# A state-space mixer with a mixture of experts: x added by an accumulating transfer, and sums of squares by four 32-column strips

## What is computed

```python
xn = layernorm(x)
zxbcdt = xn @ in_proj_w.T                    # z, xBC, dt
xBC = silu(conv_b + causal_conv4(xBC, conv_w))
theta = clip(theta_base + tanh(xn @ theta_w1) @ theta_w2)
lam = lambda_base + viscosity_eta * theta**2
# scan over chunks of 64 with state S: S_t = exp((-lam + i theta) dt) S_{t-1} + B_t x_t dt
y = real(C . S) + D * x_ssm
g = y * silu(z)
g = g * rsqrt(mean(g*g, over 512 features) + 1e-5) * norm_w
mixer = g @ out_proj_w.T
e_out = xn @ expert_w[idx] + expert_b[idx]   # idx: the router's best expert of each token
out = x + mixer + gate * e_out
```

## Time and profile before

| what | value |
|---|---|
| median of 3 runs | 1242.69 us (1236.13 to 1245.13) |
| the profiled execution's own time | 1231.05 us |
| its span in the trace | 1229.2 us |
| mean granted TensorE clock, share of full | 0.942 |
| PE busy | 1063.8 us, 87% |
| PEld busy | 826.3 us, 67% |
| DVE busy | 1044.4 us, 85% |
| ACT busy | 815.0 us, 66% |
| POOL busy | 270.0 us, 22% |
| DMA share of 16 engines, loop of the mixer | 0.44 |

### The profile page before, as it was taken

How to read it: one execution, slowest core, us unless ns; L and a number is a source line. 1 busy time by engine, 2 the same in 40 slices (tenths; PEclk the granted TensorE clock), 3 DMA queues, 4 the chain that set the end, 5 groups by cost and what they waited for, 6 DMA issues and landing times.

```text
span 1229.2 us, 26224 instructions
## 1 busy us (share of the span) xinstructions
PE 1063.8 (87%) x8826; PEld 826.3 (67%) x8827; DVE 1044.4 (85%) x1934; ACT 815.0 (66%) x1453; POOL 270.0 (22%) x307
## 2 busy tenths in 40 slices
PE   3772299846899999999999999999999999999895
PEld 2441266544677777777777777777877777777674
DVE  5757923227999999999999999999999999999962
ACT  2441211108988888887888888888888888887650
POOL 1212676600011111221111111111122111111111
PEclk9895599977899999999999999999999999999997
DMA  6993155641444444444444444444444444444341
GB/s 231 360 363 122 35 163 178 168 119 45 146 145 149 144 153 143 148 136 150 152 148 144 144 151 152 144 153 144 144 136 146 154 145 150 145 148 144 125 138 33
DMA packets 144270, 185.55 MB, mean 151 GB/s; under 512 B 20142, under 2 KB 101343, under 8 KB 143760
## 3 DMA queue, kind: packets, MB, share of 16 engines
q1 hardware_dynamic: 122736, 146.70, 35.3%
q0 software_dynamic: 6528, 17.83, 5.6%
q10 hardware_dynamic: 14880, 19.40, 4.5%
HBM read 75.99 MB, written 40.63 MB: 95 GB/s over the span
## 4 chain that ended last, share of the span: by engine, by line
DVE 51%; issue 21%; PE 2%; POOL 1%; ACT 1%; DVEq 1%; DMA 0%; POOLq 0%; ACTq 0%
DVE conv L1143 13%; DVE att L1229 4%; DVE g L1247 3%; DVE prod L1202 3%; DVE decay L1176 3%; DVE prod L1201 3%; DVE prod L1212 3%; DVE prod L1211 3%; DVE o_tile L1269 2%; DVE phase L1168 2%; DVE x_tile L1254 2%; DVE lam L1160 2%; DVE state L1237 2%; DVE cown L1216 2%; DVE theta L1151 1%
## 5 line engine op out<-in xcount | busy, mean ns | idle before, releaser
L817 PE MATMUL ps<-xn_in,win 128*128 128x256 f32 x1152 | 289.5, 393 | 25.9 <-DMA xn_in<-xnT_d 15.6
L817 PEld LDWEIGHTS ps<-xn_in,win 128*128 128x128 f32 x1152 | 214.3, 195 | 57.3 <-issue 13.6
L1143 DVE SCALAR_TENSOR_TENSOR conv<-x_pre,col,conv 128x256 f32<-128x256 f32 x480 | 195.2, 479 | 15.6 <-ACT conv L984 15.5
L942 PE MATMUL ps<-wout,g 128*128 128x256 f32 x512 | 129.5, 398 | 23.8 <-DVE o_tile L1269 23.8
L1309 POOL TENSOR_TENSOR state_in<-state,cin_s 128x256 f32<-128x256 f32 x56 | 43.4, 775 | 478.3 <-DVE state L1237 478.3
L942 PEld LDWEIGHTS ps<-wout,g 128*128 128x128 f32 x512 | 97.9, 197 | 43.2 <-issue 29.4
L1322 POOL TENSOR_TENSOR rms<-ms,cst 128x1 f32<-128x1 f32 x64 | 46.6, 729 | 245.4 <-DVE ms L1261 245.4
L631 DVE TENSOR_TENSOR r_tiles<-ps,r_expw 128x256 f32<-128x256 f32 x72 | 30.6, 425 | 79.9 <-issue 73.7
L929 PEld LDWEIGHTS ps<-att,x_tok 128*64 128x64 f32 x1024 | 54.6, 136 | 49.6 <-issue 26.5
L984 ACT ACTIVATE conv<-ps,col 128x256 f32<-128x256 f32 x160 | 83.7, 572 | 0.0
L1229 DVE TENSOR_TENSOR att<-ps,cst 128x1024 f32<-128x1024 f32 x64 | 77.2, 1207 | 5.6 <-PE ps L902 5.6
(11 more groups left out here) (169 smaller groups left out, 2338.2 us busy)
## 6 DMA issues: line engine op xcount, KB each, us to landing
cin_s<-cin SPq DMA_DIRECT2D x128, 129.0 KB, 2.2
rep<-bc_d SPq DMA_DIRECT2D x128, 128.0 KB, 2.8
grow_s<-grow SPq DMA_DIRECT2D x128, 128.0 KB, 2.1
bup_s<-bup SPq DMA_DIRECT2D x128, 128.0 KB, 2.0
cown_s<-cown SPq DMA_DIRECT2D x128, 128.0 KB, 2.0
expert_d<-r_tiles ACTq DMA_DIRECT2D x18, 512.0 KB, 3.0
xn_d<-r_tokens SPq DMA_DIRECT2D x16, 512.0 KB, 9.1
xnT_d<-r_tiles ACTq DMA_DIRECT2D x16, 512.0 KB, 7.4
```

Of the source, the lines that this page charges most:

```text
L817: last = nc.tensor.matmul(dst, win[:, kt, n * P:(n + 1) * P], xn_in[b][:, kt, :], start=(kt == 0), stop=(kt == KT - 1))
L942: nc.tensor.matmul(bank_o[:, 0:D_MODEL], g[ch][:, q, :], wout[:, q, :], start=(q == 0), stop=(q == PAIRS - 1))
L1143: nc.vector.scalar_tensor_tensor(conv[:, ct, :], x_pre[b][:, ct, tap:tap + MT], c("conv_w", ct * D_CONV + tap), conv[:, ct, :], ALU.mult, ...
```

## The change

- The DVE step `back_plus`, the SP step `load_x` and the tiles `x_tile` and `e_tile` go. `back_gather` now fetches the rows of the next macro tile into `plus_tile` (two macro tiles deep), a new ACT step `back_scale` multiplies them in place by the gate, and a new POOL step `back_add_x` issues a DMA that adds x to them in place (`accum_op=ALU.add`). `back_final` waits for that DMA.
- `back_square_sum` is cut in two. `back_square_parts` (PE) has four matmuls with 32 columns of ones as weights and the pieces of `gsq` streamed (128 columns each), into partitions 0 to 31, 32 to 63, 64 to 95 and 96 to 127 of `bank_o`. `back_parts` (ACT) copies this to `gsum`. `back_square_sum` (PE) is one matmul with `gsum` as weights and one column of ones, which adds the rows; each is there 32 times, so `back_ms` scales by 1/(32 * 512).
- All five lists are written in another order.

```diff
 sync_mixer
-                    load_xn(m + 3)
-                    stack_grow(m + 1)
-                    load_x(m)
-                    load_hidden(m + 3)
-                    load_dt(m + 3)
+                    stack_grow(m + 1)
+                    load_xn(m + 3)
                     stack_cin(m + 1)
                     stack_bup(m + 1)
                     stack_cown(m + 1)
+                    load_dt(m + 3)
+                    store(m, 0)
                     bounce(m + 2)
-                    store(m, 0)
+                    load_hidden(m + 3)
                     replicate(m + 2)
                     store(m, 1)
 tensor_mixer
+                def back_square_parts(m, ch):
+                    t = m * TPM + ch
+                    pe.wait_ge(s["squared"], t + 1)
                     for q in range(PAIRS):
-                        last = nc.tensor.matmul(bank_o[:, D_MODEL:D_MODEL + 1], gsq[:, q, :], k("ones")[:, 0:1], start=(q == 0), stop=(q == PAIRS - 1))
-                    last.then_inc(s["oproj"], 1)
+                        rows = slice(q * 32, (q + 1) * 32)
+                        last = nc.tensor.matmul(bank_o[rows, D_MODEL:D_MODEL + P], k("ones")[:, 0:32], gsq[:, q, :], start=True, stop=True)
+                    last.then_inc(s["gsum"], 1)
+                def back_square_sum(m, ch):
+                    t = m * TPM + ch
+                    pe.wait_ge(s["summed"], t + 1)
+                    nc.tensor.matmul(bank_o[:, D_MODEL + P:D_MODEL + P + 1], gsum[:, :], k("ones")[:, 0:1], start=True, stop=True).then_inc(s["oproj"], 1)
 the list of PE, now:
+   front_z_b(m+1), back_out(m,0), back_update(m,1), back_square_parts(m,0), front_turn(m+1,1), back_y(m,1),
+   front_x_a(m+3), back_square_sum(m,0), front_x_b(m+3), front_x_c(m+3), back_turn(m+1,0), back_out(m,1),
+   back_turn(m+1,1), back_update(m+1,0), back_square_parts(m,1), back_scores(m+1,0), back_square_sum(m,1),
+   front_theta(m+3), front_turn(m+2,0), front_z_a(m+2), back_y(m+1,0), back_scores(m+1,1)
 scalar_mixer
+                def back_scale(m, ch):
+                    t = m * TPM + ch
+                    act.wait_ge(e_loaded2[ch], 16 * (m + 1))
+                    tile = plus_tile[m % 2][ch]
+                    nc.scalar.activation(tile[:, :], tile[:, :], ACT.Copy, scale=gate[:, t:t + 1]).then_inc(s["xplus"], 1)
+                def back_parts(m, ch):
+                    t = m * TPM + ch
+                    act.wait_ge(s["gsum"], t + 1)
+                    after(act, s["oproj"], t)
+                    nc.scalar.activation(gsum[:, :], bank_o[:, D_MODEL:D_MODEL + P], ACT.Copy).then_inc(s["summed"], 1)
 the list of ACT, now:
+   front_trig(m+1), front_tok(m+1,0), front_skip(m+1), front_z(m+1,0), front_halo(m+3), back_scale(m+1,0),
+   front_lambda(m+2), back_square(m,0), front_bpart(m+1,0), front_bpart(m+1,1), front_z(m+1,1), back_scale(m+1,1),
+   back_parts(m,0), front_tok(m+1,1), front_silu(m+2), front_round(m+2), front_x_a(m+3), front_x_b(m+3),
+   front_x_c(m+3), back_b(m+1,0), back_square(m,1), front_exp(m+2), back_parts(m,1), back_b(m+1,1)
 vector_mixer
-                def back_plus(m, ch):
-                    nc.vector.scalar_tensor_tensor(x_tile[ch][:, :], e_tile[ch][:, :], gate[:, t:t + 1], x_tile[ch][:, :], ALU.mult, ALU.add).then_inc(s["xplus"], 1)
 the list of DVE, now:
+   front_waves(m+1), back_gate(m,0), front_cin(m+1), back_mask(m,1), front_phase(m+2), front_bup(m+1),
+   front_cown(m+1), back_ms(m,0), back_gate(m,1), back_state(m,1), front_lamdt(m+2), back_final(m,0),
+   front_decay(m+2), front_frac(m+2), front_conv(m+3, 0 to 9), front_conv(m+3, 10 to 14), back_mask(m+1,0),
+   back_ms(m,1), front_clip(m+3), back_state(m+1,0), back_final(m,1)
 gpsimd_mixer
+                def back_add_x(m, ch):
+                    t = m * TPM + ch
+                    pool.wait_ge(s["xplus"], t + 1)
+                    pool.dma_start(plus_tile[m % 2][ch][:, :], x[t * P:(t + 1) * P, :], accum_op=ALU.add).then_inc(x_loaded[ch], 16)
 the list of POOL, now:
+   back_gather(m+1,0), back_gather(m+1,1), back_state(m,0), back_rms(m,0), back_add_x(m+1,0), back_add_x(m+1,1),
+   back_state(m,1), back_rms(m,1)
```

More of the change, by code:

```diff
@@ L646, in mixer_and_experts @@
             "cquad", "dquad", "rmsd", "eidx", "statein", "repd", "tail", "apart", "signed", "lcdec", "lmasked", "lsum", "lexpd",
-            "lbdec", "lscored", "bpart", "bprod", "cprod", "eposd", "statedec", "waved", "xtok")}
+            "lbdec", "lscored", "bpart", "bprod", "cprod", "eposd", "statedec", "waved", "xtok", "gsum", "summed")}
         hidden_loaded = [sem(f"hidden_loaded{b}") for b in range(2)]
@@ L784, in load_x @@
                 @macro
[L785 to L791, removed]
                 def store(m, ch):
@@ L1106, in back_square @@
                     act.wait_ge(s["gated"], t + 1)
-                    after(act, s["oproj"], t)
+                    after(act, s["gsum"], t)
                     nc.scalar.activation(gsq[:, :, :], g[ch][:, :, :], ACT.Square).then_inc(s["squared"], 1)
@@ L1112, in scalar_mixer @@
                     front_trig(m + 1)
+                    front_tok(m + 1, 0)
+                    front_skip(m + 1)
+                    front_z(m + 1, 0)
+                    front_halo(m + 3)
+                    back_scale(m + 1, 0)
                     front_lambda(m + 2)
[L1114 to L1117, removed]
+                    back_square(m, 0)
                     front_bpart(m + 1, 0)
                     front_bpart(m + 1, 1)
-                    front_halo(m + 3)
-                    front_tok(m + 1, 0)
-                    back_square(m, 0)
+                    front_z(m + 1, 1)
+                    back_scale(m + 1, 1)
+                    back_parts(m, 0)
                     front_tok(m + 1, 1)
                     front_silu(m + 2)
+                    front_round(m + 2)
                     front_x_a(m + 3)
                     front_x_b(m + 3)
-                    front_skip(m + 2)
                     front_x_c(m + 3)
+                    back_b(m + 1, 0)
                     back_square(m, 1)
                     front_exp(m + 2)
-                    back_b(m + 1, 0)
+                    back_parts(m, 1)
+                    back_b(m + 1, 1)
             def vector_mixer(dve):
@@ L1276, in vector_mixer @@
                     front_waves(m + 1)
-                    front_lamdt(m + 2)
+                    back_gate(m, 0)
                     front_cin(m + 1)
-                    back_gate(m, 0)
-                    front_conv(m + 2, range(10, 15))
-                    back_state(m, 0)
                     back_mask(m, 1)
-                    back_plus(m, 0)
-                    front_decay(m + 2)
+                    front_phase(m + 2)
                     front_bup(m + 1)
                     front_cown(m + 1)
-                    back_plus(m, 1)
                     back_ms(m, 0)
                     back_gate(m, 1)
+                    back_state(m, 1)
+                    front_lamdt(m + 2)
+                    back_final(m, 0)
+                    front_decay(m + 2)
                     front_frac(m + 2)
-                    back_final(m, 0)
                     front_conv(m + 3, range(0, 10))
+                    front_conv(m + 3, range(10, 15))
+                    back_mask(m + 1, 0)
+                    back_ms(m, 1)
                     front_clip(m + 3)
-                    back_state(m, 1)
-                    back_ms(m, 1)
-                    front_phase(m + 3)
-                    back_mask(m + 1, 0)
+                    back_state(m + 1, 0)
                     back_final(m, 1)
@@ L1326, in gpsimd_mixer @@
                 for m in range(-BEFORE, MACROS):
-                    back_gather(m, 0)
-                    back_gather(m, 1)
+                    back_gather(m + 1, 0)
+                    back_gather(m + 1, 1)
                     back_state(m, 0)
                     back_rms(m, 0)
+                    back_add_x(m + 1, 0)
+                    back_add_x(m + 1, 1)
                     back_state(m, 1)
```

53 lines of the change are left out of this document (28 added, 25 removed).

## The result

The changed kernel is slower. Its median is 1264.63 us (four runs, 1262.04 to 1272.4) against 1241.65 for the kernel before in the same rounds, a ratio of 1.019 (95% interval 1.016 to 1.023). The forecast was 1216. Ratios leave out runs in a slower state of the chip, of which there are two, both among the ten runs of the first experiment; its median counts them. The profiled execution took 1263.76 us with a span of 1262.0, 32.8 more than before.

What follows compares the result with a forecast made beforehand. DVE was taken to bound the loop, PE close behind; 23.2 (`back_plus`) + 0 (fill) + 4 (drain) = 27.2 us off the median 1242.69 gave 1215.5, said as 1216, range 1205 to 1238.

Steps and rivals of the forecast that it cites:

- The 0.80 us of `back_plus`: DVE loses this step, 0.40 us twice an iteration; 29 x 0.80 = 23.2 us if DVE stays the bound.
- The price of the strips: Eight 32-column matmuls for the squares on PE: 0.4 us taken, bounds 0.26 to 0.91.
- the 0.56 us of exposed tails: On PE, four array-mode switches an iteration might each expose a drain tail, ending PE at 27.5; left out of the sum.
- ACT's and POOL's work as costs: ACT gets 1.4 us more, to about 25 of 27.5; POOL's accumulating DMAs taken at 1.0 us, hidden.
- the walk: Step positions in the new order, added from start-to-start distances in microseconds from an iteration's first DVE step; period 27.5 us.
- The drain: Iteration 29: z_a stands behind the scores, so the mask comes earlier; 4 us gained, bounds 0 and 7.
- The gather rival: Gather heads ACT's list and closes a chain to `front_bup`; landing at 6 us gives about 1258 us; 10%.
- the two waits: PE waits at `back_out`(m,1) for `back_final`(m,0) and at `front_theta`(m+3) for the hidden load; costed at nothing.
- a long stretch at the lower granted clock: Sign of a wrong forecast: it would turn PE's waits into lost time everywhere.
- its deadline at 26.8: POOL's `back_state`(m,1), issued behind two `back_add_x` DMAs from about 15.5, has its result needed by 26.8 us.
- The fill: First three iterations keep the same chain in another order; 0 taken, bounds 3 us either way.
- The first: PE becomes the bound if strips don't overlap or mode switches cost: period about 28.0, 1230 us; 18%.

Runs made afterwards that it cites:

- the first experiment: Changed kernel with load_hidden(m+3) issued right behind load_xn(m+3), some 14 us earlier: 1231.98 us, ratio 0.9986 to the kernel before.
- the joining step alone: Kernel before, its order and squares kept, with only new gathers, back_scale, accumulating DMAs and no back_plus or load_x: 1206.34 us, ratio 0.981.
- the early load: load_hidden(m+3) moved right behind load_xn(m+3): loop 827.0 us against the changed kernel's 848.8; with accumulating DMAs also moved early, 792.2 against 825.5.
- the strips alone: Kernel before, its order and joining of x kept, with only the squares summed by four 32-column matmuls, gsum and one matmul: 1237.31 us, ratio 1.006.
- the filler: Kernel before with only the new squares, their four 32-column matmuls of each tile issued twice: 1237.25 us, ratio 0.9975.
- the mended ones: Changed kernel, load_hidden early, plus back_add_x ahead of back_rms(m,0) (1204.09 us, 0.970) or back_state(m,1) ahead of back_add_x (1201.91 us, 0.977).

## Why the prediction was wrong

**What held.** The bound of the old kernel and its period (28.3 undisturbed). The 0.80 us of `back_plus`, shown by the joining step alone. The price of the strips, 0.36 us to the next start against 0.4, so the 0.56 us of exposed tails did not come. ACT's and POOL's work as costs: `back_scale` 0.50 us long, an accumulating DMA 1.12 on POOL, against 1.0 taken. The positions: in a period without a hole the walk was right to about a microsecond up to `back_final`(m,0). The drain gave 3.4 us up to the last `back_final`, against 4. The gather rival did not come: ACT waited 4.9 us for gathers in 20 iterations, and DVE never at `front_bup`.

**The step that failed first** is "So I cost the two waits at nothing; PE's small remaining slack hides them, and where it is gone they cost in full". In an undisturbed iteration the load was issued at 20.7 as said (741.13, with `epos` at 720.42), in the median at 21.7. It landed in 3.5 us in the median, and not in the 2.0 that it took in its old place. So the waits ran from 0.5 to 2.9 us, 1.5 in the mean, where the forecast had up to 1 and hidden. And the price of a wait on PE was missing: behind it the clock may fall, which costs PE 1.7 us more. I had the row for this, at 855.36, and read it as an accident that happens twice, not as what each such wait on a nearly full PE risks. The list of signs named "a long stretch at the lower granted clock", but the sum gave it no price; what came was 17 short ones. Once late, PE comes late at `back_gate` and `back_ms`, DVE gives the delay on, and the slack never builds up. With the other cause present the early load is worth 21.8 us of loop (848.8 to 827.0), with it removed 33.3 (825.5 to 792.2).

**The second** is "Nothing is added on DVE. The work of a period falls from 28.3 to 27.5 us". It was 28.1. Two prices of the walk were wrong, in opposite directions: the pair of decay scans cost 2.03 us in the mean and not 1.18, and the pair of phase scans 1.27 and not the 1.62 within the 2.02 for three steps. `back_state`(m,1), behind two DMAs on POOL, was checked against its deadline at 26.8 and found in time; that it would run beside a scan, and what a scan costs there, was not asked. The rows for it were in the trace of the kernel before too: `front_phase`, the same shape as `front_decay`, took 881 ns an instruction beside POOL's tensor_tensor steps and decay 676 alone (500 to 1066 us):

```profile
L1176 DVE TENSOR_TENSOR_SCAN decay<-cst,lam 128x256 f32<-128x256 f32 x40 | 25.4, 676 | 0.0
L1168 DVE TENSOR_TENSOR_SCAN phase<-cst,frac,angle 128x256 f32<-128x256 f32 x30 | 25.2, 881 | 0.0
```

The periods without a hole show 28.09 - 27.26 = 0.83 us, 24 us in the loop.

**The fill** cost 3.7 us, where I took none. PE waits 6.3 us in it for `front_clip`, behind the whole of `front_conv` in the new list, against 3.3 before, and 5.8 in its second wait for an `xn` load, against 2.8; no run parts the two.

**The rivals.** None named the mechanism. The first came nearest, PE late, but by its own work; the runs show the opposite, idle time. My chance for slower, 0.09, was too low for a change that rewrites all five lists, two of them of engines with less than 1 us to spare. The idea that the walk could be right in every position and still fail on what waits do to the clock had no chance of its own.

## What to carry to other kernels

On a nearly full PE an added wait can cost more than its length (here 0.7 us of a period by itself, 2.5 with a fall of the clock): ask of each wait on PE what stands behind it at half clock, and prefer an early load, or even filler work, to an idle microsecond. A step on POOL has two prices, its deadline and its neighbours: look at what DVE runs beside it, since here a pair of scans beside `state_in` took 1.7 times as long. And test parts in the old order and orders with the old parts: here the content was worth 2.4%, and the new lists cost 4.3% (1.019 against 0.976).

## What was not expected

- Useless matmuls made a kernel faster: 1.006 to 0.9975 of the kernel before (loop 829.5 to 821.4 us), with 0.22 us more PE work a tile, since waits of up to 1.24 us became 0.8 or less. In the kernel before, with 22 waits of 0.78 to 1.0 us at `back_out`, the clock fell twice; with the strips alone it fell behind nine of 15 waits of 1.06 to 1.24; with the filler, waits of at most 0.8, never in the loop.
- A pair of DVE scans took 2.05 us in place of 1.18 beside one POOL tensor_tensor, which itself took 1.56 where it takes 0.62 beside `back_mask` in the kernel before and 1.00 ahead of the scans in the mended ones; two accumulating DMAs issued beside the same scans cost them nothing.
- The same 48 KB load took 2.0 us from issue to landing in the median early in the iteration of the old list, 2.8 behind `load_xn` in the new list and 3.5 behind `load_dt`, `store` and `bounce` there.
